# Two graph layers on one core: four sets of one-hots and sums in flight instead of two, a ring of 64 gathered tiles instead of 128, and turn tables that VectorE writes in SBUF

## The reference

```python
def _seg_mean(vals, idx, num_nodes):
    s = segment_sum(vals, idx); cnt = segment_sum(ones, idx)
    return s / maximum(cnt, 1.0)[:, None]
feat_in  = h @ W_in.T + b_in;   feat_out = h @ W_out.T + b_out
a_in  = _seg_mean(feat_in[src], dst, N)      # sums over a node's sources
a_out = _seg_mean(feat_out[dst], src, N)     # and over its destinations
h = gru_cell(concat(a_in, a_out), h, w_ih, w_hh, b_ih, b_hh)
x = layernorm(x + h)
```

## Time and profile before

| | us |
|---|---|
| median of 3 runs (lowest, highest) | 8651.19 (8642.64, 8704.52) |
| the profiled execution, its own time | 8592.66 |
| its span in the profile | 8591.0 |
| GpSimd busy in the span | 5270.2 (61%) |
| TensorE busy | 4860.7 (57%) |
| VectorE busy | 3136.4 (37%) |
| ScalarE busy | 1682.3 (20%) |

### The profile page before, as it was taken

One profiled execution on the slowest core, in us unless ns is written; L12 is line 12 of the kernel. 1 busy time (PEld: TensorE's weight loads), 2 busy tenths in 40 slices (PEclk: granted clock), 3 DMA queues, 4 the chain that ended last, 5 costly groups with the idle time before them and its releaser, 6 DMA issues.

```text
span 8591.0 us, 115667 instructions
## 1 busy us (share of the span) xinstructions
PE 4860.7 (57%) x27117; PEld 4156.9 (48%) x27117; DVE 3136.4 (37%) x6639; ACT 1682.3 (20%) x4659; POOL 5270.2 (61%) x6008
## 2 busy tenths in 40 slices
PE   5888888888888899122232322323344444444337
PEld 4777777777777799122222322323233333333333
DVE  7555555555555567111111311112111111111128
ACT  2222222222223366100000000000111111111006
POOL 2556555555655676656666666665666666666654
PEclk7666667676767799566666666666666666666668
DMA  3222223222222598222222122221222222222225
GB/s 107 91 90 97 93 90 96 92 93 93 95 91 93 170 310 276 67 43 46 46 46 46 42 46 46 47 47 37 55 63 62 64 62 63 62 64 62 51 60 159
DMA packets 903626, 722.39 MB, mean 84 GB/s; under 512 B 601771, under 2 KB 703782, under 8 KB 902874
## 3 DMA queue, kind: packets, MB, share of 16 engines
q1 hardware_dynamic: 628082, 338.08, 14.6%
q0 software_dynamic: 161968, 341.31, 13.7%
q10 hardware_dynamic: 113469, 41.94, 1.9%
HBM read 556.95 MB, written 170.31 MB: 85 GB/s over the span
## 4 chain that ended last, share of the span: by engine, by line
another core or an unknown queue 34%; issue 11%; PE 9%; ACTq 4%; DVE 3%; ACT 2%; DVEq 2%; DMA 1%; POOL 0%; SPq 0%; POOLq 0%
PE bank L1966 5%; PE bank L2015 2%; DVE acc_b L1656 1%; ACTq L418 1%; DVEq L418 1%; DMA arena<-blktab 1%; ACTq L1035 1%; DVE acc_a L396 0%; ACT arena L1052 0%; ACTq L1066 0%; ACT acc_a L1014 0%; ACTq L1038 0%; DVE arena L1650 0%; PE bank L2071 0%
## 5 line engine op out<-in xcount | busy, mean ns | idle before, releaser
L821 POOL DMA_INDIRECT arena<-x1d,edge x3322 | 3142.5, 946 | 1741.9 <-issue 968.8
L2015 PE MATMUL bank<-arena 128*128 x8256 | 1438.7, 346 | 2245.4 <-DVE acc_b L1656 1575.9
L2015 PEld LDWEIGHTS bank<-arena 128*128 128x128 f32 x8256 | 1369.7, 257 | 2345.2 <-issue 2326.9
L762 POOL DMA_INDIRECT msgs<-arena x1664 | 1646.3, 989 | 1249.3 <-DVE arena L1436 774.5
L1650 DVE TENSOR_TENSOR arena<-bank,arena 128x1024 f32<-128x1024 f32 x516 | 631.2, 1224 | 3893.1 <-remote 3289.5
L1052 ACT ACTIVATE arena<-edge,arena 128x4 f32 x1032 | 224.7, 286 | 3159.7 <-issue 2951.4
L1916 PE MATMUL bank<-w2s,acc_b 128*128 128x128 f32 x3328 | 744.7, 392 | 20.1 <-issue 19.7
L1916 PEld LDWEIGHTS bank<-w2s,acc_b 128*128 128x128 f32 x3328 | 631.0, 282 | 160.6 <-issue 160.6
L1899 PE MATMUL bank<-arena 128*128 (+1 forms) x3328 | 662.8, 352 | 76.4 <-issue 72.8
L1899 PEld LDWEIGHTS bank<-arena 128*128 128x128 f32 x3328 | 585.5, 258 | 95.1 <-issue 92.6
L1401 DVE TENSOR_TENSOR_SCAN acc_b<-arena,acc_b 128x512 f32<-128x512 bf16 x415 | 531.7, 1281 | 7.4
(11 more groups left out here) (320 smaller groups left out, 5334.4 us busy)
## 6 DMA issues: line engine op xcount, KB each, us to landing
arena<-msgs SPq DMA_DIRECT2D x512, 272.0 KB, 4.9
arena<-rows SPq DMA_DIRECT2D x208, 512.0 KB
arena<-x1d,edge POOLq DMA_INDIRECT x3322
msgs<-arena POOLq DMA_INDIRECT x1664
pred<-arena ACTq DMA_DIRECT2D x98, 256.0 KB
arena<-pred SPq DMA_DIRECT2D x12, 1792.0 KB, 8.5
arena<-xwin SPq DMA_DIRECT2D x208, 64.0 KB
arena<-in_edge_attr_dram SPq DMA_DIRECT2D x207, 32.0 KB
```

The costliest lines, as they stand in the source:

```text
L762: pool.indirect_dma_start(msgs, bass.IndirectOffsetOnAxis(ap=pos[:, b, j:j + 1], axis=0), mrow[:, b, j, :], None).then_inc(scattered[b], 16)
L821: pool.indirect_dma_start(grow_t[:, sl, 0:D], None, x1d, bass.IndirectOffsetOnAxis(ap=edge2[:, odd * RING + sl, 1:2].bitcast(i32), axis=0) ...
L2015: last = mm(sum_at(q, u), oh1[:, q % 2, u * UT + k, :], rows[:, k * CW:(k + 1) * CW], start=(k == 0), stop=(k == UT - 1))
```

## The change

Four one-hot sets can be in flight instead of two: `DEPTH` = 4 one-hot buffers and PSUM areas (banks 0 to 3), so that VectorE waits for set n-4 before it makes set n, and adds the sums of two turns back. The ring has 64 slots (GR = 8 groups), so that GpSimd may be 8 groups ahead of the counted sums, SyncE looks 4 groups back, and the edge list's buffer holds 128 tiles instead of 256. All turns' table rows are written by VectorE straight into an SBUF table (`turn_tab`, with `unit_blk` for the block offsets), so the 24 copies to DRAM, ScalarE's two loads per turn and the waits for both are gone. The number of gathers, one-hot sets, matmuls and additions is unchanged. The core of the diff:

```diff
-RING = 128
+RING = 64
-SW = 4 * NU + TU
+SW = 3 * NU + 1 + TU
+DEPTH = 2 * TU
-        oh1 = cut(2 * TG * P).rearrange("p (b s n) -> p b s n", b=2, s=TG)
-        blk_now = cut(2 * NU).rearrange("p (s k) -> p s k", s=2)
+        oh1 = cut(DEPTH * TG * P).rearrange("p (b s n) -> p b s n", b=DEPTH, s=TG)
+        turn_tab = cut(V1 // NU * SW, i32)
+        unit_blk = cut(V1)
...
-            return bank[q % 2 * 3][:, k * CW:(k + 1) * CW]
+            return bank[q][:, k * CW:(k + 1) * CW]
+        def turn_row(it, at, n):
+            return turn_tab[0:1, bass.ds(it * SW + at, n)]
...
-            def pair_table(half):          # SyncE: 6 DMAs for each of 2 chunks
...
-            pair_table(0)
-            for i in range(2):
-                sp.wait_ge(pair_copied[i], PAIR_ROWS * (CHUNKS // 2))
+            sp.wait_ge(s["pair_out"], CHUNKS)
...
+            def ring_round(r, odd, last=False):
+                gathers(r, odd, lambda i: r * GR + i - (GR - 1), last)
...
+            for half in range(2):
+                first = half * rounds + 1 - half
+                pairs = (rounds - 2 + half) // 2
+                with pool.Fori(0, pairs) as c:
+                    for i in range(2):
+                        ring_round(2 * c + first + i, (first + i) % 2)
+                for r in range(first + 2 * pairs, (half + 1) * rounds):
+                    ring_round(r, r % 2, r == (half + 1) * rounds - 1)
...
-            def turn(half, it, n, loads):
...
-                need(act, s["oh1_ready"], half * V1 // UG + (0 if first else it - 1) * TU)
-                if not isinstance(it, int) or it >= 2:
-                    act.wait_ge(s["sum1_ready"], half * V1 // UG + it * TU - 2 * TU + 1)
-                part = slice(NU if first else 0, NU if last else SW)
-                act.dma_start(turntab[:, slot, part], sumtab[half:half + 1, bass.ds(it, 1), part].rearrange("o t k -> o (t k)")).then_inc(turn_in[slot], 16)
...
-                act.dma_start(blk_now[:, slot, :], blktab[half, bass.ds(it, 1), :].to_broadcast([P, NU])).then_inc(turn_in[slot], 16)
+            def turn(half, it, slot):
+
+                need(act, s["oh1_ready"], half * V1 // UG + (it - 1) * TU)
...
-                act.wait_ge(turn_in[slot], loads)
...
-                    last_key = nc.scalar.activation(key_now[:, slot, k * UT:(k + 1) * UT], keys, ACT.Identity, bias=blk_now[:, slot, k:k + 1])
+                    last_key = nc.scalar.activation(key_now[:, slot, k * UT:(k + 1) * UT], keys, ACT.Identity, bias=unit_blk[:, bass.ds(it * NU + k, 1)])
...
-            def sums1(half, it, slot, loads, made=True, added=True):
+            def sums1(half, it, slot, made=True, added=True):
...
-                v0, first = half * V1 + (it - 1) * NU, half * V1 // UG + it * TU
+                v0, first = half * V1 + (it - 2) * NU, half * V1 // UG + it * TU
...
                 for q in range(TU):
+                    b = slot * TU + q
                     if added:
-                        dve.wait_ge(s["sum1_ready"], first + q - 1)
+                        dve.wait_ge(s["sum1_ready"], first + q - DEPTH + 1)
...
-                pe.wait_ge(turn_in[slot], loads)
...
-                    need(pe, s["add1_done"], half * V1 + it * NU + (q - 1) * UG)
+                    need(pe, s["add1_done"], half * V1 + it * NU + (q - DEPTH + 1) * UG)
```

More of the change, by code:

```diff
@@ L635, in _ @@
                 round_of(r, r % 2, int(r == rounds - 1))
-            pair_table(1)
-            with sp.Fori(rounds // 2, rounds - 2) as c:
-                for odd in (1, 0):
-                    round_of(2 * c + (2 - odd), odd, 1, lambda chunk: dlist[bass.ds((chunk - GL) * (NT * P), NT * P), :])
-            for r in range(2 * rounds - 3, 2 * rounds):
+            sp.wait_ge(s["pair_out"], 2 * CHUNKS)
+            pairs = (rounds - 3) // 2
+            with sp.Fori(0, pairs) as c:
+                for i in range(2):
+                    round_of(2 * c + rounds + i, (rounds + i) % 2, 1, lambda chunk: dlist[bass.ds((chunk - GL) * (NT * P), NT * P), :])
+            for r in range(rounds + 2 * pairs, 2 * rounds):
                 round_of(r, r % 2, 1)
@@ L1614, in pair_table @@
                 for c in range(CHUNKS):
-                    n, at, w = half * CHUNKS + c, c * HCHUNK, min(HCHUNK, V1 - c * HCHUNK)
-                    row = lambda r: pairrow[0:1, c % 2, r, 0:w]
+                    at, w = c * HCHUNK, min(HCHUNK, V1 - c * HCHUNK)
+                    entry = lambda a, n: turns_of[:, at // NU:(at + w) // NU, a:a + n]
+                    by_turn = lambda of, n: of.rearrange("o (t k) -> o t k", k=n)
+                    quads = by_turn(quad_i[0:1, 0:w], NU)
+                    keys, rows, tiles, lists = entry(NU + 1, NU), entry(2 * NU + 1, NU), entry(3 * NU + 1, TU), entry(NU, 1)
@@ L1630, in pair_table @@
-                    us.link(v.tensor_scalar(row(5), row(5), float(1 + half * (GL - T % LISTS // NT)), None, ALU.add))
+                    us.mark(v.tensor_scalar(keys, quads, LISTS // UT - 1, (2 * UT).bit_length() - 1, ALU.bitwise_and, ALU.logical_shift_left))
+                    us.mark(v.tensor_scalar(rows, quads, RING // UT - 1, None, ALU.bitwise_and))
+                    us.mark(v.tensor_scalar(tiles, quads.rearrange("o t (q u) -> o t q u", u=UG)[:, :, :, UG - 1], (TG // UT).bit_length() - 1, None, ALU.logical_shift_right))
```

142 lines of the change are left out of this document (44 added, 98 removed).

## The result

| | before | after |
|---|---|---|
| median, us | 8653.43 (4 runs, 8642.64 to 8704.52) | 8570.60 (4 runs, 8564.12 to 8572.98) |
| profiled execution, us | 8592.66 (span 8591.0) | 8564.12 (span 8562.5) |
| ratio after / before | | 0.9892, 95% interval 0.9852 to 0.9931 |

The change gains 83 us (60 to 128 by the interval) where 209 were forecast. The two profiled executions differ by only 28.5 us, because the one of before lies 58.5 us under its own median; the traces can explain the smaller number, and they show where the waits lie.

The account below looks back on a forecast made before the run. The prediction took GpSimd, waiting for a full ring because sums are reported late, to bound the kernel. Terms -143 - 74 - 5 - 25 + 8 + 5 + 25 = -209 us gave 8442 us from 8651.19; range 8200 to 8690 us.

Parts of the forecast that it names:

- a finished sum is reported to the others with a delay of ten to twenty-odd us: Neighbour sums: while GpSimd gathers, finished sums are reported ten to twenty-odd us late; a pause of GpSimd releases them.
- I take two more per pause: 2.86 + 2 = 4.86: Neighbour sums, first half: four sets in flight give 4.86 sets per GpSimd pause, 36.9 fewer pauses, -143 us.
- 16 to 24: Sign of a wrong forecast: GpSimd's runs stay at 16 to 24 gathers, so counts, not buffers, set the pace.
- the half weight that the prediction gave to this fear: Second half: TensorE's waits for ScalarE may remain despite more sets, so half of -148 us was taken, -74.
- Middle: Between the halves: tables in SBUF remove VectorE's 4.66 us wait for the copies, -5 us.
- Tail: After the last gather: a ring of 64 leaves 9.9 sets less to catch up, -25 us.
- Turns of GpSimd's loops: GpSimd's loops over two rounds turn 24 times instead of 10: +28 us at most, +25 taken.
- the +8: Start of the neighbour sums: the smaller ring halves GpSimd's first run without a pause, +8 us.
- The number of sets doesn't matter: Rival, neighbour sums: TensorE itself is slow during gathers, so a pause releases no more than now; 8659 us, chance 0.20.
- GpSimd is never held up: Rival, neighbour sums: sums get ahead of gathers, the ring isn't full, all but the middle stall goes; 7974 us, chance 0.10.
- TensorE runs out of tiles: Rival, neighbour sums: SyncE reports tiles too late for TensorE, cutting sets per pause to 2.0; 8925 us, chance 0.15.
- the forecast's own stretch: Whole kernel: some of GpSimd's pauses gone, 8308 to 8569 us, chance 0.55.

Follow-up runs that it names:

- experiment 2: Changed kernel plus a register operation before table waits, then with two sets, or half the matmuls, undisturbed chip: 7278.79, 7276.72, 7278.21 us; kernel before 7279.89.
- experiments 3, 4, 5: No kernel: test sections on eight cores, matmuls beside streams, then gather pitches; slow die 961.9 to 981.4 us, 922.5 us median; 480 matmuls 134 us back to back.
- experiment 6: Changed kernel plus a register operation before table waits, disturbed chip (kernel before 8644.86 us): two sets 8619.75 us, ratio 0.9962; half the matmuls 8505.17 us, 0.9826.
- experiment 7: Neighbour sums' loop alone with constants, varying depth, ring and matmuls: disturbed means 546 to 553 us a variant; three variants with 96 sets 1134, 1127, 1120 us.

## Why the prediction was wrong, step by step

*What bounds.* Right for the chip that was measured: GpSimd, held up behind the freeing of the ring, in 174 pieces. On an undisturbed chip the same kernel has no such wait (experiment 2).

*The failed step: "a finished sum is reported to the others with a delay of ten to twenty-odd us", and from it "I take two more per pause: 2.86 + 2 = 4.86".* The delay isn't a lateness of a set as a whole, from which a pause releases all that is in flight. It is a price per instruction: under back-to-back gathers a matmul passes every 2.8 us (experiments 3, 4, 5), so a set takes some 44 us, 21 with half the matmuls (experiment 6), however many stand ready. After a pause TensorE runs at full rate for some ten us, and what fits in there is let through. More sets ready fill that stretch better, and that gave 0.64 sets more per pause in the first half (3.50 instead of 2.86) where 2 were taken, and none in the second (2.63 instead of 2.66). The runs between pauses had 1306/58 = 22.5 gathers, where 31.5 were forecast and "16 to 24" stood as the sign of being wrong. Whether the instructions themselves or only their counts are held stays open (experiment 7). By the counts the first half gave 1661/1306 x 58 = 73.8 pauses of 267.1/58 - 0.3 = 4.31 us, 318 us, against 89.6 x 3.88 = 348: -30 where -143 stood. The second half gave 97.8 x 3.69 = 361 against 346: +15 where -74 stood. There TensorE's waits for ScalarE (`x_t`, `pre_lin`) grew from 412 to 494 us (6300 to 8100 us), which fits the half weight that the prediction gave to this fear; no run tested it.

*The smaller terms.* Middle: -15 instead of -5. Tail: -38 instead of -25. Turns of GpSimd's loops: the short idle grew by 984.5 - 968.8 = 15.7 us, of which 12 more pieces are 4; so +12 instead of +25. The first stop came at 3590.96 instead of 3642.85, 13.52 us long instead of 4.72; but up to 3700 us GpSimd waited 23.3 us for the ring against 24.5, so the +8 doesn't show. A term that the prediction didn't have: the gathers themselves took 3152.6 us instead of 3142.5. The whole stage, read directly, went from 3457.93 to 8394.07 before and from 3477.29 to 8366.1 after, -47 us: the waits for the ring -35 (768.5 to 733.4, the middle's -15 in it), the short idle +16, the gathers +10, the tail -38. Ahead of the stage this pair of traces lost 19 us, with the untouched scatter stage's waits 20 us longer, and so the profiled times differ by -28.5. The rest of the median's -83 lies in how far the profiled execution of before stands under its own median, and isn't explained by a row.

*The rivals.* "The number of sets doesn't matter" was nearest to the mechanism, and its counter-argument failed: the blocks of 32 records in 5.28 us were in a full-rate stretch, and said nothing on the next 30 us. Its time, 8659, was wrong, as it gave depth nothing and the tail too little. It had 0.20; the rows at the stage's start, one set per 44 us with no pause near, would have given it more. "GpSimd is never held up" is what an undisturbed chip does, with any depth. "TensorE runs out of tiles" didn't occur: no wait of TensorE for tiles among its leading ones.

*The direction* was right. That the range held the time is luck in good part: 8570.6 lies just above the forecast's own stretch (8308 to 8569) and below that of no change (8620 to 8690), and over the 8565 under which 0.65 had been put; and the largest gain of the traces came from the tail, not from the sets in flight.

## What to carry to other kernels

When a consumer seems to be told late, look for a stretch in which the producer beside it never pauses, and divide: if the distance of two results is the number of recorded instructions times one constant, and halves with half the instructions, it is a price per instruction and no fixed lateness. Buffers then buy only what fits in the fast stretches. What is left are fewer instructions on the slowed engine (half the matmuls, with half the sums' terms left out, gave a ratio of 0.9826 where the change gave 0.9892) and the pitch of the gathers, which costs GpSimd's own time (0.27 us a gather) and was not tried in the kernel on a disturbed core. Before tuning to such a wait, run the kernel on another chip: here the same kernel took 1370 us less on it, and the change was worth nothing.

## What the runs showed of the hardware

- On some dies, TensorE's records show a matmul (with its weight load) every 2.80 us (2.91 on two of four cores), and VectorE and ScalarE an instruction every 1.40 us, while GpSimd issues indirect DMAs 1.25 us apart. It begins after a stretch at full rate (4.6 us with 41 bf16 matmuls, 36 us with 80 records of 512-wide float32 ones), hits bf16 128 columns and float32 512 columns alike, straight code and loop alike; it is partly there at a pitch of 1.51 us (480 matmuls in 40 to 96 us) and gone at 1.75. SyncE's DMAs, GpSimd's direct DMAs and its arithmetic don't cause it. On the other die of the same chip, with the same program at the same time, it isn't there.
- It went with the die, not the program: of the four chips that were seen with all cores, two had the first die disturbed and two the second, none both or neither. Two chips came up at two times each, with core 0 undisturbed both times.
- Each run here was recorded by the profiler, on disturbed and undisturbed dies alike, so recording alone isn't the cause; that it has a part can't be excluded, as no run was without it. The kept traces speak for a part: with the same program, they hold far fewer semaphore events on disturbed cores (the kernel with two sets: 42772 updates on the disturbed chip, 124456 on an undisturbed one; the model of experiment 7: 7872 to 9624 on cores 0 to 3, 36537 to 39088 on cores 4 to 7), while the instruction records are as many. So what is disturbed takes in the way of the records. It also means that on a disturbed core the engine named behind a wait, or the word "issue", is less sure. The Trainium skill (NOTIFIC — Programmer's Manual, section 1.1, The problem) has the engine that reports an event already moved on while the record is written; if the steps of 1.40 us are such reports, that doesn't hold on a disturbed die. No run here shows what the steps are.
